# Normalising the turned x on GpSimd from a second, already turned input, in an attention and feed-forward block

## The reference

```python
def reference(x, Wqkv, Wo, weight, aux_weight1, aux_weight2, bias):   # x: 32 x 256 x 128, f32
    x = x + layernorm(attention(layernorm(x), Wqkv, Wo))
    x = x + layernorm(tanh(layernorm(x) @ weight @ aux_weight1 @ aux_weight2 + bias))
    return x
# attention: H = 8 heads, D = 64; q and k get a sinusoidal position table; scores / 8, causal mask,
# softmax, times v; heads put together; times Wo.T
# layernorm: (x - mean) / sqrt(var + 1e-5) over the last axis (128), without weights
```

## Time and profile before

| what | value |
|---|---|
| median of 3 runs | 534.92 us (533.73 to 535.1) |
| the profiled execution | 533.72 us |
| its span | 531.5 us |
| PE busy | 509.8 us (96%) |
| DVE busy | 457.2 us (86%) |
| ACT busy | 433.8 us (82%) |
| POOL busy | 394.9 us (74%) |
| granted TensorE clock | 0.994 of full speed |
| DMA | 23.26 MB, mean 44 GB/s |

### The profile page before, as it was taken

How to read it: one execution, slowest core, us unless ns; L and a number is a source line. 1 busy time by engine, 2 the same in 40 slices (tenths; PEclk the granted TensorE clock), 3 DMA queues, 4 the chain that set the end, 5 groups by cost and what they waited for, 6 DMA issues and landing times.

```text
span 531.5 us, 17273 instructions
## 1 busy us (share of the span) xinstructions
PE 509.8 (96%) x5336; PEld 419.9 (79%) x5336; DVE 457.2 (86%) x2061; ACT 433.8 (82%) x1604; POOL 394.9 (74%) x650
## 2 busy tenths in 40 slices
PE   6989999999999999999999999999999999999984
PEld 2778888888888888888888888888888888888762
DVE  3788889988889998888999888899988889998754
ACT  2688888988888888888888888888988888898831
POOL 4454578877777887777788777778877777886664
PEclk9899999999999999999999999999999999999999
DMA  5020112111211211121121112112111211211000
GB/s 168 17 56 23 26 47 51 33 46 47 51 41 43 53 31 47 47 51 41 43 51 33 46 45 53 41 42 52 34 45 47 51 41 42 53 24 29 22 21 20
DMA packets 64991, 23.26 MB, mean 44 GB/s; under 512 B 34819, under 2 KB 64390, under 8 KB 64902
## 3 DMA queue, kind: packets, MB, share of 16 engines
q1 hardware_dynamic: 63942, 21.45, 16.6%
q10 hardware_dynamic: 960, 0.72, 0.4%
HBM read 14.03 MB, written 8.13 MB: 42 GB/s over the span
## 4 chain that ended last, share of the span: by engine, by line
PE 86%; POOL 4%; issue 4%; DVE 3%; ACT 1%; DMA 1%; SPq 0%; POOLq 0%; DVEq 0%; ACTq 0%
PE turned_and_heads L1120 16%; PE scores L1063 16%; PE misc_bank L1186 12%; PE turned_and_heads L1106 11%; PE qk_bank L1081 7%; PE qk_bank L1082 5%; PE qk_bank L1083 5%; PE misc_bank L1049 4%; PE misc_bank L1050 2%; PE misc_bank L1051 2%; PE misc_bank L1159 2%; PE misc_bank L1126 2%; PE misc_bank L1157 1%; DMA x_in<-in_x 1%; ACT probs L323 1%
## 5 line engine op out<-in xcount | busy, mean ns | idle before, releaser
L323 ACT ACTIVATE probs<-scores,neg_max 128x256 f32<-128x256 f32 (+1 forms) x512 | 209.8, 436 | 11.6 <-DVE neg_max L742 11.0
L742 DVE CUSTOM_DVE_ANT_0 scores<-scores,mask 128x256 f32<-128x256 f32 (+1 forms) x512 | 165.3, 388 | 10.6 <-PE scores L1063 8.9
L518 POOL TENSOR_TENSOR probs<-probs,inv_sum 128x512 f32<-128x512 f32 x126 | 103.1, 839 | 16.3 <-DVE inv_sum L760 16.3
L323 ACT ACTIVATION_READ_ACCUMULATOR probs<-scores,neg_max 128x1 f32 x512 | 113.4, 221 | 0.0
L352 ACT COPY pt<-turned_and_heads 128x512 f32<-128x512 f32 x128 | 75.4, 589 | 37.3 <-PE turned_and_heads L1106 36.9
L1063 PE MATMUL scores<-qk 64*128 64x256 f32 (+1 forms) x1024 | 99.9, 334 | 1.1 <-ACT probs L323 0.9
L1120 PE MATMUL turned_and_heads<-pt,vals 128*64 128x256 f32 (+1 forms) x1024 | 97.3, 332 | 0.8 <-ACT pt L354 0.5
L1063 PEld LDWEIGHTS scores<-qk 64*128 64x128 f32 x1024 | 84.4, 190 | 8.8 <-issue 1.8
L1120 PEld LDWEIGHTS turned_and_heads<-pt,vals 128*64 128x64 f32 x1024 | 63.8, 136 | 33.9 <-issue 11.9
L754 DVE TENSOR_TENSOR qk<-qk_bank,pe 128x512 f32<-128x512 f32 x128 | 86.0, 672 | 3.0 <-PE qk_bank L1083 2.6
L1081 PE MATMUL qk_bank<-xt_hi,w_hi 128*128 128x256 f32 x256 | 81.5, 318 | 2.5 <-DVE xt_lo L789 2.4
(11 more groups left out here) (95 smaller groups left out, 906.3 us busy)
## 6 DMA issues: line engine op xcount, KB each, us to landing
x_in<-in_x SPq DMA_DIRECT2D x32, 128.0 KB, 2.3
x_res<-in_x SPq DMA_DIRECT2D x32, 128.0 KB, 2.2
out_x<-x SPq DMA_DIRECT2D x32, 128.0 KB, 2.1
x_rows<-x_blocks SPq DMA_DIRECT2D x120, 32.0 KB, 2.0
xt<-x_rows SPq DMA_DIRECT2D x30, 128.0 KB, 2.3
w_raw<-in_w_qkv_t SPq DMA_DIRECT2D x2, 256.0 KB, 5.0
w_raw<-in_w_qkv_t ACTq DMA_DIRECT2D x1, 256.0 KB, 4.9
pe<-pe_table SPq DMA_DIRECT2D x1, 256.0 KB, 5.6
```

The source lines that it names most:

```text
L323: ins = nc.scalar.activation(probs[k][j][:, h, lo:hi], s_bank[j][:, h, lo:hi], ACT.Exp, bias=neg_max[k][j][:, i:i + 1], scale=-1.0, accum_ ...
L518: ins = nc.gpsimd.tensor_tensor(some, some, inv, ALU.mult)
L742: ins = nc.vector.tensor_tensor_reduce(some, some, mask[:, t * P:2 * P], -1.0, HIGHEST, ALU.add, ALU.min, neg_max[k][j][:, i:i + 1])
```

## The change

The host gives the kernel x a second time as `x_t`, with the axes exchanged to features, batch, tokens. From batch 2 on, x is no longer normalised before it is turned:

- SP's `load_raw` loads x turned but not normalised into x_raw. `load_x` of batches from 4 on waits for the stats of x and not for the normalised xn.
- POOL's `norm_x` makes only rstd, and writes it into the place of the variance in `moments`, so that mean and rstd of every token lie side by side.
- SP's `send_x` writes `moments` (four numbers a partition) to DRAM in one DMA, and `read_x`, now right behind it in slot 0, reads these 512 numbers back to all 128 partitions as x_all (2 KB a partition).
- POOL's new `norm_raw` subtracts the mean and multiplies by rstd, which now vary along the row: of x_all it reads every fourth number. It stands behind the second scale_probs and ahead of rstd_attn.
- DVE's `turn_x_blocks` goes, and so do the four DMAs of blocks.
- `keep_x_hi` waits for norm_raw; DVE's stats of x wait for the send of the batch before.

```diff
+        x_rows = [nc.dram_tensor(f"x_rows{i}", [P, TT * 2], F32, kind="Internal").ap() for i in range(2)]
...
+            def load_raw(b):
+                if not b.exists() or b.is_below(2):
+                    return
+                wait(sp, raw_centered, b.times(1, -3))
+                sp.dma_start(x_raw[b.parity][:, :, :], x_t[:, b.times(1), :].rearrange("e (t p) -> e t p", t=TT)
+                             ).then_inc(raw_loaded[b.parity], 16)
...
             def send_x(b):
-                sp.wait_ge(x_blocked, b.times(1, -1))
-                send(b, x_blocks, x_rows, x_sent)
+                sp.wait_ge(norms["x"]["rstd_made"], b.times(1, 1))
+                wait(sp, x_moved[b.parity], (moves(b, 2) - 1) * 16)
+                sp.dma_start(x_rows[b.parity], norms["x"]["moments"][:, :, :].rearrange("p t k -> p (t k)")
+                             ).then_inc(x_sent[b.parity], 16)
             def read_x(b):
-                sp.wait_ge(x_sent[b.parity], moves(b, 2) * 64)
-                sp.dma_start(xt[b.parity][:, :, :], x_rows[b.parity]).then_inc(x_moved[b.parity], 16)
+                sp.wait_ge(x_sent[b.parity], moves(b, 2) * 16)
+                wait(sp, raw_normed, b.times(1, -3))
+                sp.dma_start(x_all[b.parity][:, :, :, :].rearrange("q p t k -> q (p t k)"),
+                             x_rows[b.parity].rearrange("p c -> (p c)").unsqueeze(0).to_broadcast([P, P * TT * 2])
+                             ).then_inc(x_moved[b.parity], 16)
...
                 if k == 0:
                     load_x(b.plus(3))
+                    load_raw(b.plus(2))
                     send_x(b.plus(2))
+                    read_x(b.plus(2))
                 else:
-                    read_x(b.plus(2))
                     store(b.plus(-3))
                     load_res(b.plus(1))
...
+                if b.is_below(2) and not b.is_first():
+                    normalise("x", b, x_in[b.parity], xn[b.parity])
+
+            def norm_raw(b):
+                if not b.exists() or b.is_below(2):
+                    return
+                to = xt[b.parity]
+                mean, rstd = (x_all[b.parity][:, :, :, k].rearrange("q p t -> q t p") for k in range(2))
+                pool.wait_ge(raw_loaded[b.parity], moves(b, 2) * 16)
+                pool.wait_ge(x_moved[b.parity], moves(b, 2) * 16)
+                pool.wait_ge(x_lo_kept, b.times(1, -1))
+                nc.gpsimd.tensor_tensor(to[:, :, :], x_raw[b.parity][:, :, :], mean, ALU.subtract).then_inc(raw_centered, 1)
+                pool.wait_ge(raw_centered, b.times(1, -1))
+                nc.gpsimd.tensor_tensor(to[:, :, :], to[:, :, :], rstd, ALU.mult).then_inc(raw_normed, 1)
...
                     scale_probs(b, 1)
+                    norm_raw(b.plus(2))
                     rstd_attn(b.plus(-1))
...
                     take_moments("ffn", b.plus(-3))
-                    turn_x_blocks(b.plus(2))
                     keep_qk(b.plus(1), 0, 1)
```

More of the change, by code:

```diff
@@ L63, in constants, with build_block @@
     return np.ascontiguousarray(pe_qk), np.ascontiguousarray(mask), np.eye(P, dtype=np.float32)
-def build_block(nc, x, w_qkv_t, w_o_t, w1_t, w2, w3, bias, out, H):
+def build_block(nc, x, x_t, w_qkv_t, w_o_t, w1_t, w2, w3, bias, out, H):
     B, T, E = x.shape
@@ L120, in two @@
             return [sb(f"{name}{i}", shape, dt) for i in range(2)]
-        def two_dram(name):
-            return [nc.dram_tensor(f"{name}{i}", [P, TT, E], F32, kind="Internal").ap() for i in range(2)]
         x_in, x_res = two("x_in", [P, TT, E]), two("x_res", [P, TT, E])
@@ L128, in build_block @@
         xt_hi, xt_lo = two("xt_hi", [P, T], F32R), two("xt_lo", [P, T], F32R)
-        x_blocks, x_rows, xt = two("x_blocks", [P, TT, E]), two_dram("x_rows"), two("xt", [P, TT, E])
+        x_raw, xt, x_all = two("x_raw", [P, TT, P]), two("xt", [P, TT, P]), two("x_all", [P, P, TT, 2])
+        x_rows = [nc.dram_tensor(f"x_rows{i}", [P, TT * 2], F32, kind="Internal").ap() for i in range(2)]
         vals = two("vals", [P, TT, F])
@@ L160, in build_block @@
         x_turned, x_hi_kept, x_lo_kept = sem("x_turned"), sem("x_hi_kept"), sem("x_lo_kept")
-        x_blocked, x_sent, x_moved = sem("x_blocked"), [sem(f"x_sent{i}") for i in range(2)], [sem(f"x_moved{i}") for i in range(2)]
+        raw_loaded, x_sent, x_moved = ([sem(f"{n}{i}") for i in range(2)] for n in ("raw_loaded", "x_sent", "x_moved"))
+        raw_centered, raw_normed = sem("raw_centered"), sem("raw_normed")
         attn_made, attn_kept, x1_made, out_made = sem("attn_made"), sem("attn_kept"), sem("x1_made"), sem("out_made")
@@ L223, in load_x @@
                     return
-                wait(sp, norms["x"]["normed"], b.times(1, -1))
+                sp.wait_ge(norms["x"]["normed" if b.is_below(4) else "stats_taken"], b.times(1, -1))
                 load(b, x_in, x_loaded)
+            def load_raw(b):
[4 more added lines that the diff above has]
+                             ).then_inc(raw_loaded[b.parity], 16)
             def load_res(b):
@@ L233, in load_res @@
                 load(b, x_res, res_loaded)
[L235 to L240, removed]
             def send_x(b):
@@ L362, in keep_x_hi @@
                 else:
-                    wait_moved(act, b, x_moved, 2)
+                    act.wait_ge(raw_normed, b.times(1, -1))
                 wait(act, qk_made, pairs(b, -2, 0))
@@ L492, in make_rstd @@
                 pool.wait_ge(n["moments_taken"], b.times(1, 1))
-                wait(pool, n["normed"], b.times(1))
+                rstd = n["rstd"][:, :]
+                if name == "x" and not b.is_below(2):
+                    rstd = n["moments"][:, :, 1]
+                    pool.wait_ge(n["rstd_made"], b.times(1))
+                else:
+                    wait(pool, n["normed"], b.times(1))
                 nc.gpsimd.tensor_tensor(n["var_eps"][:, :], n["moments"][:, :, 1], eps[:, :], ALU.add
@@ L497, in make_rstd @@
                 pool.wait_ge(n["eps_added"], b.times(1, 1))
-                nc.gpsimd.tensor_tensor(n["rstd"][:, :], n["var_eps"][:, :], half_power[:, :], ALU.pow
+                nc.gpsimd.tensor_tensor(rstd, n["var_eps"][:, :], half_power[:, :], ALU.pow
                                         ).then_inc(n["rstd_made"], 1)
@@ L623, in begin @@
                 norm_x(first.plus(3))
+                norm_raw(first.plus(2))
                 scale_probs(first, 1)
                 scale_probs(first.plus(1), 0)
+                norm_raw(first.plus(3))
                 scale_probs(first.plus(1), 1)
@@ L632, in begin @@
                 scale_probs(first.plus(2), 1)
+                norm_raw(first.plus(4))
                 rstd_attn(first.plus(1))
@@ L672, in take_stats @@
                 n = norms[name]
-                wait(dve, n["normed"], b.times(1))
+                if name == "x" and not b.is_below(3):
+                    before = b.plus(-1)
+                    dve.wait_ge(x_sent[before.parity], moves(before, 2) * 16)
+                else:
+                    wait(dve, n["normed"], b.times(1))
                 for t in range(TT):
@@ L790, in keep_x_lo @@
                                         xt_hi[b.parity][:, :].bitcast(F32), ALU.subtract).then_inc(x_lo_kept, 1)
[L792 to L799, removed]
             def slot(b, k):
@@ L926, in begin @@
                 row_max(first, 1, 0)
-                turn_x_blocks(first.plus(2))
                 keep_qk(first.plus(1), 0, 0)
@@ L940, in begin @@
                 stats_x(first.plus(4))
-                turn_x_blocks(first.plus(3))
                 keep_qk(first.plus(1), 1, 1)
@@ L970, in begin @@
                 keep_qk(first.plus(3), 0, 0)
-                turn_x_blocks(first.plus(4))
                 keep_heads(first.plus(1), 1)
@@ L1331 @@
         "x": L0_attn_x,
+        "x_t": _np.asarray(L0_attn_x).transpose(2, 0, 1),
         "w_qkv_t": w_qkv_t,
```

6 lines of the change are left out of this document (removed).

## The result

The changed kernel takes 551.28 us (median of 4 runs, 550.26 to 551.9), the kernel before 535.01 (4 runs). The ratio is 1.031, with a 95% interval of 1.0285 to 1.033: 3.1% slower. The profiled execution took 551.29 us with a span of 549.0, so it stands for the median. 545.4 was forecast, with a range of 534 to 557. Of the four runs of the first variant with neighbouring numbers, further down, one took 688.14 us at a granted clock of 0.65 and is left out; the other three took 542.75 to 544.12.

The account below looks back on a forecast made before the run. PE was taken to set the cycle at 15.45 us; POOL's round of 13.98 + 1.87 = 15.85 adds 10.8 us over 27 slots, less 0.3 at the start, giving 545.4 us against the median, range 534.0 to 557.0.

Parts of the forecast that it names:

- POOL's round decides: Repeating slots: norm_raw's two operations lengthen POOL's round to 15.85 us, 0.40 above PE's 15.45, in 27 slots, 10.8 us.
- attn_var_eps to y_var_eps: First piece of POOL's round: 5.02 us falls to 4.66, as DVE's 0.28 us wait for PE's scores goes.
- the correction: POOL's scale_probs and ffn_var_eps take longer when DVE's L770 starts earlier: 0.09 us a batch, range 0 to 0.18.
- the pair: norm_raw's two POOL operations, between the second scale_probs and attn_var_eps: 2d + 0.04 us.
- d: Duration of one norm_raw operation on POOL, which reads every fourth number: 0.94 us.
- the two bounds: Limits for one norm_raw operation: 0.61 us below, 1.14 above, as if the read paid for all 512 numbers.
- The numbers' way through DRAM: x_all lands by 291.3 at the latest and norm_raw wants it at 293.4: 2 us of cover, no cost.
- keep_x_hi wants the result of norm_raw most of a batch later: The later xt in the repeating slots was costed at nothing.
- The gain at the start: In the start the block transpose lies on the last chain once, with 0.34 us: a gain of 0.3 us.
- The rival on the other side: norm_raw's read with gaps costs no more than L580, round 15.44, time 534.6 or 533.7 us; chance 0.24.
- PE's floor: PE's work is untouched, so its 15.45 us a batch can't be undercut.

Follow-up runs that it names:

- first variant with neighbouring numbers: Changed kernel with norm_raw reading its mean and rstd operands as 256 neighbouring numbers of x_all, not those needed: 542.79 us, ratio 1.014.
- The kernel before with the pair added: Kernel before plus two POOL operations of norm_raw's form on scratch data ahead of rstd_attn in 27 slots: 547.15 us, ratio 1.022.
- the run with the transpose put back: Changed kernel with DVE's block transpose back in its old place in the slots, on data nobody reads: 545.43 us, ratio 1.018.
- planes: Changed kernel with the y_stats wait behind the row maximum and mean and rstd sent to DRAM as 512 single numbers of 4 bytes: 616.83 us, ratio 1.152.
- the DVE variants: Changed kernel with norm_raw's times-rstd operation on DVE behind x's moments: 558.48 us, ratio 1.042; with the y_stats wait moved as well 558.01, 1.040.
- the kernel before with only the moved wait: Kernel before with DVE's wait for y_stats moved from ahead of the row maximum to behind it: 534.85 us, ratio 0.999.
- the wait moved: Changed kernel with DVE's wait for its own y_stats moved behind the row maximum, directly ahead of y_moments: 537.99 us, ratio 1.004.
- pairs: Changed kernel with the y_stats wait behind the row maximum and mean and rstd sent to DRAM as 256 pieces of 8 bytes: 532.83 us, ratio 0.995.
- the one with the operation earlier on DVE: Changed kernel with the y_stats wait moved and the times-rstd operation on DVE behind attn's moments, ahead of the heads copy: 539.08 us, ratio 1.008.

## Why the prediction was right, step by step

**POOL's round decides: right.** It was forecast slower because two operations fill POOL's only slack while the removed ones had covered a wait for y_moments. The marks came: attn_moments waited for no more, a wait for y_moments of 1.33 us a batch (about 1 was said), attn_rstd waited for 0.90 a batch (over 0.7 was said), and PE waiting inside scores. Two sizes were off, norm_raw's operations (0.94 said) and the round (15.85 said). The kernel before with the pair added shows the cause alone.

**The terms of the round.** 15.85 us was forecast and 16.06 measured, and 545.4 against 551.3. The measured pieces are means of 27 batches, and the errors partly cancel:

| piece | forecast | measured |
|---|---|---|
| attn_var_eps to y_var_eps | 4.66 | 4.95 |
| y_var_eps to the end of scale_probs, with the correction | 9.28 | 9.33 |
| the pair | 1.91 | 1.78 |

The first row is the term that failed. The sum took 0.28 us off because "DVE waited for PE's scores", as the profile's idle note said. The wait was DVE's for its own y_stats, it did not go with a late POOL, and moving it gave back 0.3 us a batch and, since DVE's scale_probs then came later, 0.15 more. The second is the correction for the two scale_probs: 0.09 was taken, the middle of 0 to 0.18, and 0.15 was measured, the 9.33 against the 9.18 of the run with the transpose put back. The 0.18 taken from the earlier trace rows, 0.17 by the rows themselves, left out ffn_rstd behind them, which gives 0.06 back (0.69 in place of 0.75). The third is d: 0.94 forecast, 0.87 measured, inside the two bounds and nearer to L580. With the three measured terms the sum gives the measured round. Part of the closeness is luck: with d right and the other two terms as they were, the forecast would have been 13.98 + 1.74 = 15.72 us a batch and 541.9 us, 7 us above the kernel before where 16.3 were measured. The price d that was set too high made up for a part of the first term.

**What was costed at nothing.** The numbers' way through DRAM was covered, as said: x_all lands 3.6 us after its issue and POOL never waits for it in the repeating slots. It had about 4.7 us to spare (294.12 + 3.6 to 302.43), where 2 was said. With planes the cover broke and POOL stood at norm_raw as described, at a price of about 80 us. But the sentence "keep_x_hi wants the result of norm_raw most of a batch later" was wrong. POOL runs norm_raw at the end of its round, when ACT is already at the next batch's xt_hi, and ACT waits 0.33 us in 23 batches. The trace of before had this in it: ACT starts an xt_hi at 294.86, 0.23 us behind the attn_var_eps of 294.63 ahead of which the pair was to stand. The wait is not on the chain in the changed kernel, but 0.9 us of it made the DVE variants 4% slower than before. The row of before:

```profile
294.86 0.42 ACT L367 CAST xt_hi<-xt 128x256 fp32r<-128x256 f32 x1
```

**The gain at the start** of 0.3 us did not show. The second attn_var_eps is at 62.65 before and 63.48 after; but it is at 63.45 in the kernel before with only the moved wait, whose start is the same. The load of the second batch landed after 6.68 us in place of 6.14, and the granted clock between 12 and 20 us was 0.66 after and 0.79 before (0.66 also in the kernel before with the moved wait). 0.3 us can't be told apart from this.

**The rival on the other side** (a plain read, not slower) was decided at d = 0.735. The run with neighbouring numbers has d = 0.73 and is still 1.4% slower, because the first term was 0.3 too short. With the wait moved, which brings that term to 4.63, the decision holds: pairs at d = 0.74 are at PE's pace.

**PE's floor** of 15.45 us was not one. PE's work was untouched, and the run with pairs had a round of 15.38.

## What to carry to other kernels

Work that leaves an engine's queue was worth nothing where it stood in front of a wait for another engine, and work that enters it costs in full where it takes the last slack of a loop that passes over other engines; so sum the loop piece by piece, and not the busy shares. Where an idle note names an engine that had long been done, look in the program for the wait that stands there: one wait on an engine's own result was worth 13 us once its loop set the pace. And when the layout of small numbers is chosen, weigh the pieces of the transfer against the step of the read: 8 bytes was cheap on both sides here.

## What the runs showed of the hardware

- A GpSimd tensor_tensor of 256 f32 numbers a partition with two full operands took 0.73 us with a step of 4 bytes in one operand, 0.74 with 8, and 0.87 with 16.
- A GpSimd tensor_tensor of 256 numbers took 1.08 us in place of 0.61 when a DVE instruction with two SBUF operands started just ahead of it. The GpSimd pair that it belongs to took 2.06 to 2.14 us with the DVE start 0.84 to 0.99 us behind its own, and 1.61 with the start 1.07 us or more behind, in every trace. The two GpSimd instructions after it were 0.27 and 0.06 us shorter in return, so the net was 0.15 us a batch. 0.41 us of DVE work that nobody needs moved the start and saved 4.6 us in 27 batches.
- A DVE row maximum started 0.69 us after the start of y_stats with a wait for the end of y_stats between them, and 0.39 to 0.40 without it.
- Sends to DRAM of the same 2 KB held the waiting queue for 1.8 us in 128 pieces of 16 bytes (53.5 over 30), 3.1 in 256 of 8, and 7.7 in 512 of 4.
- In the trace of the changed kernel TensorE's last attention part (L1137, 16 matmuls) took 2.69 us at a granted clock of 0.50, the lower level of 1.2 GHz, where in the kernel before it took 1.52 at 1.00 (2.4 GHz), with the same instructions at the same distances ahead of it. It took 1.52 in four of the traces, the padded kernel before and the one with the operation earlier on DVE among them, and 2.34 to 2.83 in all others; why is left open.
